# The carry of the causal convolution between two halves: made from PSUM in the first half and entered as the bias of ACT's first tap

## The chip, the cores and the metric

The kernel runs on one core of one Trainium2 chip. The metric is the device time of one execution in microseconds (us); lower is better. The engines are TensorE (PE; its weight loads are PEld), VectorE (DVE), ScalarE (ACT), GpSimd (POOL) and SyncE (SP), which issues most of the DMAs.

## The reference

One layer on 1024 tokens of 512 features, in float32: adaptive layer norm, a Mamba-2 block with 128 heads of 64 and 8 groups, its gated and normed output projection, and then a layer norm with a feed-forward product by the signs of the weights. What matters here is the causal convolution of four taps over tokens, one filter per channel, on x (8192 channels) and on B and C (1024 channels each):

```python
proj = jnp.einsum('bsd,ed->bse', x, in_proj_w)
gate = proj[..., :INTER]
hBC = proj[..., INTER:INTER + CONV_DIM]
xc = jnp.transpose(hBC, (0, 2, 1))
xc = jax.lax.conv_general_dilated(xc, conv_w, (1,), [(K - 1, 0)], ..., feature_group_count=CONV_DIM)
xc = xc + conv_b[None, :, None]
hBC = jax.nn.silu(jnp.transpose(xc, (0, 2, 1)))
hs, Bm, Cm = ...
...
Y = (Y_diag + Y_off).reshape(b, s, H, P) + hs * D[None, None, :, None]
g = y * jax.nn.silu(gate)
```

Token t of a channel becomes w3 x[t] + w2 x[t-1] + w1 x[t-2] + w0 x[t-3] + bias.

## The kernel before, in words

Channels lie on the 128 partitions, tokens along the free dimension. The 1024 tokens are two halves of 512 (HALF), and the 8192 channels of x are 16 blocks of 512 (four tiles of 128 channels, j = 0 to 3). A **unit** is one block and one half. A group holds two blocks, so four units: c = 0 (first block, first half), c = 1 (first block, second half), c = 2 and c = 3 (the second block). The 8 groups run as a loop on each engine, with the first and last written apart. All engines run programs of their own, ordered by semaphores; the order on each engine is written out by hand.

A product of float32 values is made from high and low parts, as three matmuls for each of 4 slices: one projection of a tile is 12 matmuls of 128x512 (`split_product`, lines 449 to 451) into one bank of PSUM.

The work is pipelined by a unit. While unit u computes decays, states and outputs in four steps j, TensorE also projects the four tiles of x for unit u + 1 (`project_step`), and ACT and DVE convolve them. So a unit on a first half (c = 0, 2) convolves the second half of its block, and a unit on a second half (c = 1, 3) the first half of the next block. With c = 3 also four items of the next group's B and C go with them (bc0 and bc1: B, first and second half; bc2 and bc3: C). For an item:

- ACT's `tap` (lines 828 and 838) reads the bank and writes the first tap, w3 x + bias, over all 512 columns into xc (or bt, craw). For a first half it also copies the last three columns of the bank into `tail` or `bctail` (lines 827, 837). It waits for the projection and for line 1329, which reads the old xc (`v_t2`).
- DVE's `conv` (line 1118) adds three wide taps out of the bank, of 511, 510 and 509 columns. In a second half it adds three short taps of 1, 2 and 3 columns from `tail`: what the last three tokens of the first half contribute. Each operation waits for the one before (`v_taps`), as they write the same tensor.
- ACT applies SiLU to xc (line 926), and TensorE transposes it for the next unit (line 648).

In each step j DVE does: two multiplications of lm by the mask (line 1304, after ACT's decays of lines 980 and 983), yt (1329, after TensorE's product of line 734), ea (1334), the low part of g of the step before (1311), and the convolution of item j. POOL follows with yt (1487, after ea), the gate (1490), the sum of squares (1482) and the low part of one weight tile (1418). ACT splits weights (810), copies ea (988), makes g's high part (1000) and the squares (1007), and evicts the gates with SiLU (939).

Of the gate projections (`gate_proj`), that of tile 0 for the next unit stands in step j = 2, after the last tile of x. Tiles 1 and 2 open the next unit: tile 1 waits for the third convolution (`v_conv`, as its bank is the one of that item), tile 2 for the SiLU of tile 0, and the transposes for the SiLU of all four tiles of xc. The output projection of the unit before follows the first transposes.

## Time and profile before

| what | value |
| --- | --- |
| median of 3 runs | 1948.02 us (1947.24 to 1951.38) |
| span of the profiled execution | 1944.2 us |
| time of the profiled execution with what lies around the span | not given apart; the median is 3.8 us above the span |
| TensorE busy | 1828.1 us, 94% |
| DVE busy | 1392.7 us, 72% |
| ACT busy | 1011.6 us, 52% |
| POOL busy | 925.6 us, 48% |
| mean granted clock of TensorE | 0.981 |
| DMA | 114.18 MB, mean 59 GB/s |

The span runs from the first to the last instruction. The busy time of TensorE is modelled at its ends, so 94% does not mean that it works at its peak. In the rows below an instruction is given as line, engine, operation, output<-inputs by the program's names, and shape. "[1.78 <-DVE xc L1118]" is idle time of the engine before it and what ended that. Times in a timeline are us from the start of the span, and neighbours of one kind are merged (x3), so their length is that of the row from first start to last end.

### The profile page before, as it was taken

How to read it: one execution, taken by the hardware profiler on the slowest of the kernel's cores; microseconds unless marked ns; L12 is line 12 of the kernel's file. 1: busy time of each engine (PE TensorE's matmuls, PEld its weight loads, DVE VectorE, ACT ScalarE, POOL GpSimd, SP SyncE). 2: the span in 40 equal slices, each digit the busy share in tenths (PEclk: the TensorE clock that was granted, in tenths of full speed). 3: DMA queues.
4: the chain of work that ended last, by engine and by line, in shares of the span. 5: the costliest groups of instructions: out<-in, count | busy, mean ns of one | idle time of the engine just before them, and what ended most of it. 6: DMA issues, size and time to landing. Idle time of an engine off the chain costs nothing.

```text
span 1944.2 us, 31172 instructions
## 1 busy us (share of the span) xinstructions
PE 1828.1 (94%) x9752; PEld 1410.3 (73%) x9752; DVE 1392.7 (72%) x2094; ACT 1011.6 (52%) x1775; POOL 925.6 (48%) x717
## 2 busy tenths in 40 slices
PE   7899999999999989999999999999999999999966
PEld 6767777777777768677777777777677777777745
DVE  5876677767766677866677677666777667776788
ACT  5455544555645555555445555455555555455532
POOL 1245454545534464454545545354554545454564
PEclk9799999999999999999999999999999999999988
DMA  5412121111202121021211212111211212111121
GB/s 180 154 32 69 53 63 42 46 60 50 66 30 69 44 65 50 28 69 53 63 43 45 61 44 69 32 64 47 67 50 29 64 59 63 42 46 60 33 88 58
DMA packets 76397, 114.18 MB, mean 59 GB/s; under 512 B 21696, under 2 KB 27328, under 8 KB 75328
## 3 DMA queue, kind: packets, MB, share of 16 engines
q1 hardware_dynamic: 58656, 80.07, 13.7%
q10 hardware_dynamic: 17568, 31.99, 4.9%
q8 instruction: 86, 1.41, 0.3%
q14 instruction: 87, 0.71, 0.1%
HBM read 88.94 MB, written 23.07 MB: 58 GB/s over the span
## 4 chain that ended last, share of the span: by engine, by line
PE 40%; DVE 21%; issue 19%; POOL 11%; ACT 6%; DMA 1%; SPq 0%; POOLq 0%; DVEq 0%; ACTq 0%
DVE xc L1118 11%; PE bank L449 9%; PE bank L451 9%; PE bank L450 9%; PE bank L586 3%; POOL yt L1487 3%; POOL wg_lo L1418 3%; PE bank L734 2%; POOL wx_lo L1418 2%; PE bank L648 2%; PE bank L601 1%; PE bank L721 1%; ACT lm L980 1%; PE bank L612 1%; DVE ea L1334 1%
## 5 line engine op out<-in xcount | busy, mean ns | idle before, releaser
L1487 POOL TENSOR_TENSOR yt<-yt,ea 128x384 f32<-128x384 f32 (+1 forms) x128 | 189.6, 1481 | 464.8 <-DVE ea L1334 464.8
L1118 DVE SCALAR_TENSOR_TENSOR xc<-bank,bpar,xc 128x511 f32<-128x511 f32 (+2 forms) x384 | 286.1, 747 | 43.4 <-ACT xc L838 34.2
L449 PE MATMUL bank<-h_hi,wg_hi 128*128 128x512 f32 x640 | 265.5, 415 | 39.3 <-DVE xc L1118 36.1
L1304 DVE TENSOR_TENSOR lm<-lm,cbm 128x512 f32<-128x512 f32 x256 | 173.3, 718 | 164.9 <-ACT lm L983 164.9
L451 PE MATMUL bank<-h_hi,wg_lo 128*128 128x512 f32 x640 | 255.3, 399 | 0.0
L450 PE MATMUL bank<-h_lo,wg_hi 128*128 128x512 f32 x640 | 255.0, 398 | 0.0
L449 PE MATMUL bank<-h_hi,wx_hi 128*128 128x512 f32 x512 | 211.1, 412 | 2.5 <-DVE bt L1118 1.3
L449 PE MATMUL bank<-wo_hi,g_hi 128*128 128x512 f32 x496 | 206.4, 416 | 0.0
L1468 POOL TENSOR_TENSOR prev<-prev,dec 128x512 f32<-128x512 f32 x96 | 101.9, 1061 | 215.0 <-DVE prev L1253 131.8
L450 PE MATMUL bank<-h_lo,wx_hi 128*128 128x512 f32 x512 | 201.4, 393 | 0.0
L451 PE MATMUL bank<-h_hi,wx_lo 128*128 128x512 f32 x512 | 200.9, 392 | 0.0
L451 PE MATMUL bank<-wo_hi,g_lo 128*128 128x512 f32 x496 | 194.9, 393 | 0.0
L450 PE MATMUL bank<-wo_lo,g_hi 128*128 128x512 f32 x496 | 193.6, 390 | 0.0
L939 ACT ACTIVATE gate<-bank 128x512 f32<-128x512 f32 x128 | 75.2, 588 | 210.7 <-PE bank L451 97.8
L988 ACT ACTIVATE ea<-bank 128x512 f32<-128x512 f32 x128 | 76.3, 596 | 202.4 <-PE bank L612 163.5
L449 PEld LDWEIGHTS bank<-h_hi,wg_hi 128*128 128x128 f32 x640 | 123.7, 193 | 75.4 <-DVE xc L1118 43.3
L1490 POOL TENSOR_TENSOR yt<-yt,gate 128x512 f32<-128x512 f32 x128 | 166.1, 1298 | 10.0
L1482 POOL TENSOR_TENSOR ssq<-ssq,sq 128x512 f32<-128x512 f32 x112 | 145.1, 1295 | 26.3 <-ACT sq L1007 26.3
L838 ACT ACTIVATE xc<-bank,bpar 128x512 f32<-128x512 f32 x128 | 99.4, 776 | 102.8 <-DVE yt L1329 59.3
L983 ACT ACTIVATE lm<-lm 128x512 f32<-128x512 f32 x256 | 148.9, 644 | 0.0
L734 PE MATMUL bank<-lm,xdt 128*64 128x128 f32 x2048 | 140.9, 280 | 6.8 <-DVE acc L1223 6.3
L451 PEld LDWEIGHTS bank<-h_hi,wg_lo 128*128 128x128 f32 x640 | 123.5, 193 | 28.1
(180 smaller groups left out, 3858.0 us busy)
## 6 DMA issues: line engine op xcount, KB each, us to landing
raw_w<-w_in_dram SPq DMA_DIRECT2D x145, 256.0 KB, 2.6
raw_w<-w_out_dram SPq DMA_DIRECT2D x64, 256.0 KB, 2.6
part_d<-part ACTq DMA_DIRECT2D x64, 256.0 KB, 2.4
part<-part_d ACTq DMA_DIRECT2D x58, 256.0 KB, 2.7
rt<-rows_d SPq DMA_DIRECT2D x256, 8.0 KB
acc<-x_dram SPq DMA_DIRECT2D x8, 256.0 KB, 6.8
acc<-w_mod_dram SPq DMA_DIRECT2D x2, 1024.0 KB, 6.5
lh<-neg_d SPq DMA_DIRECT2D x128, 8.0 KB
```

Of the source, the lines that this page charges most:

```text
L449: nc.tensor.matmul(out_ap, whi(k), hhi(k), start=(k == 0), stop=False)
L450: nc.tensor.matmul(out_ap, whi(k), hlo(k), start=False, stop=False)
L451: last = nc.tensor.matmul(out_ap, wlo(k), hhi(k), start=False, stop=(k == n - 1))
L734: lst = nc.tensor.matmul(bank[5][64 * i:64 * i + 64, chunk(z)], xdt[:, z, h * HDIM:(h + 1) * HDIM], lm[:, h % 4, chunk(z)], start=True, st ...
L838: act(xc[:, j, :], bank[b][:, :], ACT.Identity, bias=par(parity, j, CONV_B), scale=par(parity, j, TAPS - 1)).then_inc(a_tap, 1)
L983: act(lm[:, h % 4, :], lm[:, h % 4, :], ACT.Exp, scale=-1.0).then_inc(a_l, 1)
L1118: stt(dst[:, at], src, w(k), dst[:, at], ALU.mult, ALU.add)\
L1304: tt(lm[:, h % 4, :], lm[:, h % 4, :], cbm[:, toks(hf)], ALU.mult).then_inc(v_m, 1)
L1468: tt(prev[:, slot(hf, z + 1), :].rearrange("p (h c) -> p h c", h=BH), prev[:, slot(hf, z), :].rearrange("p (h c) -> p h c", h=BH), d.unsqu ...
L1482: tt(ssq[:, hf, :], ssq[:, hf, :], sq[:, :], ALU.add).then_inc(p_ss, 1)
L1487: tt(yt[:, j % 2, cols], yt[:, j % 2, cols], ea[:, j % 2, cols], ALU.add).then_inc(p_t3, 1)
L1490: tt(yt[:, j % 2, :], yt[:, j % 2, :], gate[:, j, :], ALU.mult).then_inc(p_g, 1)
```

## The change

In the first half DVE itself now makes from the bank what the last three tokens add to the first three of the second half, with the bias: w0 x on three columns (a tensor_scalar with the bias), then w1 x on two and w2 x on one, each interleaved with a wide tap. In the second half ACT makes the first tap of columns 0, 1 and 2 one at a time, with that column of `tail` as per-partition bias, and then the other 509 columns with the plain bias. ACT's copy of three columns is gone, and so are DVE's three short taps of the second half. ACT's tap of a second half gets a wait for the convolution of the same tile in the first half. The counters of links between DVE's operations change with the order (`taps_before`, `BC_TAPS`).

```diff
--- before.py
+++ after.py
@@ -186,10 +186,10 @@
             return 7 * nb + 4 * hf
 
         def taps_before(nb, hf, j):
-            return 28 * nb + (8 + 5 * j if hf else 2 * j)
+            return 28 * nb + (20 + 2 * j if hf else 5 * j)
         def squares_before(g, c):
             return 14 * g + (0, 3, 6, 10)[c]
-        BC_TAPS = (0, 2, 7, 9)
+        BC_TAPS = (0, 5, 7, 12)
 
 
         W_SLOTS = {"x": (wx_hi, wx_lo), "g": (wg_hi, wg_lo), "o": (wo_hi, wo_lo)}
@@ -823,9 +823,14 @@
                     if j == 0:
                         se.wait_ge(d_bcpar, 16 * (gg + 1))
                         ge(se, t_st, 14 * gg)
-                    if h2 == 0:
-                        act(bctail[:, m, :], bank[b][:, HALF - 3:HALF], ACT.Copy)
-                    act((bt, craw)[m][:, toks(h2)], bank[b][:, :], ACT.Identity, bias=bcp(m, CONV_B),
+                    o, first = (bt, craw)[m][:, toks(h2)], 0
+                    if h2 == 1:
+                        se.wait_ge(v_bcconv, 4 * gg + j)
+                        first = TAPS - 1
+                        for t in range(first):
+                            act(o[:, t:t + 1], bank[b][:, t:t + 1], ACT.Identity, bias=bctail[:, m, t:t + 1],
+                                scale=bcp(m, TAPS - 1))
+                    act(o[:, first:HALF], bank[b][:, first:HALF], ACT.Identity, bias=bcp(m, CONV_B),
                         scale=bcp(m, TAPS - 1)).then_inc(a_bctap, 1)
                     return
                 v = 2 * nb + hf
@@ -833,9 +838,14 @@
                 if j == 0 and hf == 0:
                     se.wait_ge(d_bpar, 16 * (nb + 1))
                 ge(se, v_t2, 4 * (v - 1) + j + 1)
-                if hf == 0:
-                    act(tail[:, j, :], bank[b][:, HALF - 3:HALF], ACT.Copy)
-                act(xc[:, j, :], bank[b][:, :], ACT.Identity, bias=par(parity, j, CONV_B),
+                first = 0
+                if hf == 1:
+                    se.wait_ge(v_conv, 4 * (v - 1) + j + 1)
+                    first = TAPS - 1
+                    for t in range(first):
+                        act(xc[:, j, t:t + 1], bank[b][:, t:t + 1], ACT.Identity, bias=tail[:, j, t:t + 1],
+                            scale=par(parity, j, TAPS - 1))
+                act(xc[:, j, first:HALF], bank[b][:, first:HALF], ACT.Identity, bias=par(parity, j, CONV_B),
                     scale=par(parity, j, TAPS - 1)).then_inc(a_tap, 1)
 
             def scale_h(s, scale, shift, halves=(0, 1)):
@@ -1109,14 +1119,22 @@
                     ve.wait_ge(a_tap, 4 * v + j + 1)
                     done, link, n0 = v_conv, v_tap, taps_before(nb, hf, j)
                 ps = bank[b]
-                steps = [(slice(3 - k, HALF), ps[:, 0:HALF - 3 + k], k) for k in (2, 1, 0)]
-                if h2:
-                    steps += [(slice(0, 3 - k), tl[:, k:3], k) for k in (2, 1, 0)]
-                for r, (at, src, k) in enumerate(steps):
-                    if r:
-                        ve.wait_ge(link, n0 + r)
-                    stt(dst[:, at], src, w(k), dst[:, at], ALU.mult, ALU.add)\
-                        .then_inc(done if r == len(steps) - 1 else link, 1)
+                for r, k in enumerate((2, 1, 0)):
+                    if h2:
+                        if r:
+                            ve.wait_ge(link, n0 + r)
+                    else:
+
+                        n = 3 - r
+                        if r:
+                            ve.wait_ge(link, n0 + 2 * r - 1)
+                            stt(tl[:, 0:n], ps[:, HALF - n:HALF], w(r), tl[:, 0:n], ALU.mult, ALU.add).then_inc(link, 1)
+                            ve.wait_ge(link, n0 + 2 * r)
+                        else:
+                            ts(tl[:, 0:n], ps[:, HALF - n:HALF], w(r), w(CONV_B), ALU.mult, ALU.add).then_inc(link, 1)
+                    at = slice(3 - k, HALF)
+                    stt(dst[:, at], ps[:, 0:HALF - 3 + k], w(k), dst[:, at], ALU.mult, ALU.add)\
+                        .then_inc(done if r == 2 else link, 1)
 
 
             acc_tile = lambda t: acc[:, t, :]
```

### How instructions move

DVE, second half, in the first unit of the program (c = 0), step j = 1, before. The rows are instructions in program order; `t_yd`, `a_tap` and so on are the semaphores waited for; `tail` holds the last three tokens of the first half, `bpar` the weights of the convolution. Line 1329 makes yt, line 1334 ea, line 1311 the low part of g, line 1118 is the convolution:

```order
L1329 SCALAR_TENSOR_TENSOR yt<-xc,bpar,bank 128x512 [waits t_yd]
L1334 TENSOR_TENSOR ea<-bank,ea 128x384 [waits a_ea,t_yo]
L1311 SCALAR_TENSOR_TENSOR g_lo<-yt,bpar,g_hi 128x512 [waits a_hi]
L1118 SCALAR_TENSOR_TENSOR xc<-bank,bpar,xc 128x511 [waits a_tap]
L1118 SCALAR_TENSOR_TENSOR xc<-bank,bpar,xc 128x510 [waits v_taps]
L1118 SCALAR_TENSOR_TENSOR xc<-bank,bpar,xc 128x509 [waits v_taps]
L1118 SCALAR_TENSOR_TENSOR xc<-tail,bpar,xc 128x1 [waits v_taps]
L1118 SCALAR_TENSOR_TENSOR xc<-tail,bpar,xc 128x2 [waits v_taps]
L1118 SCALAR_TENSOR_TENSOR xc<-tail,bpar,xc 128x3 [waits v_taps]
L1304 TENSOR_TENSOR lm<-lm,cbm 128x512 [waits a_l] x2
```

The same place now (the lines are 1347, 1352, 1329, 1136 and 1322 in the changed file):

```order
L1347 SCALAR_TENSOR_TENSOR yt<-xc,bpar,bank 128x512 [waits t_yd]
L1352 TENSOR_TENSOR ea<-bank,ea 128x384 [waits a_ea,t_yo]
L1329 SCALAR_TENSOR_TENSOR g_lo<-yt,bpar,g_hi 128x512 [waits a_hi]
L1136 SCALAR_TENSOR_TENSOR xc<-bank,bpar,xc 128x511 [waits a_tap]
L1136 SCALAR_TENSOR_TENSOR xc<-bank,bpar,xc 128x510 [waits v_taps]
L1136 SCALAR_TENSOR_TENSOR xc<-bank,bpar,xc 128x509 [waits v_taps]
L1322 TENSOR_TENSOR lm<-lm,cbm 128x512 [waits a_l] x2
```

The three short taps on `tail` behind the wide ones are gone, and the next multiplication of lm follows the last wide tap.

DVE, first half, in the second unit (c = 1), step j = 0, before:

```order
L1329 SCALAR_TENSOR_TENSOR yt<-xc,bpar,bank 128x512 [waits v_lo,a_sq,t_yd]
L1334 TENSOR_TENSOR ea<-bank,ea 128x512 [waits a_ea,t_yo]
L1118 SCALAR_TENSOR_TENSOR xc<-bank,bpar,xc 128x511 [waits a_tap]
L1118 SCALAR_TENSOR_TENSOR xc<-bank,bpar,xc 128x510 [waits v_taps]
L1118 SCALAR_TENSOR_TENSOR xc<-bank,bpar,xc 128x509 [waits v_taps]
L1304 TENSOR_TENSOR lm<-lm,cbm 128x512 [waits a_l] x2
```

and now:

```order
L1347 SCALAR_TENSOR_TENSOR yt<-xc,bpar,bank 128x512 [waits v_lo,a_sq,t_yd]
L1352 TENSOR_TENSOR ea<-bank,ea 128x512 [waits a_ea,t_yo]
L1134 TENSOR_SCALAR tail<-bank,bpar 128x3 [waits a_tap]
L1136 SCALAR_TENSOR_TENSOR xc<-bank,bpar,xc 128x511
L1131 SCALAR_TENSOR_TENSOR tail<-bank,bpar,tail 128x2 [waits v_taps]
L1136 SCALAR_TENSOR_TENSOR xc<-bank,bpar,xc 128x510 [waits v_taps]
L1131 SCALAR_TENSOR_TENSOR tail<-bank,bpar,tail 128x1 [waits v_taps]
L1136 SCALAR_TENSOR_TENSOR xc<-bank,bpar,xc 128x509 [waits v_taps]
L1322 TENSOR_TENSOR lm<-lm,cbm 128x512 [waits a_l] x2
```

A short operation that makes or adds to `tail` stands ahead of each wide tap, and the first of them takes the wait for ACT's tap.

ACT, second half, in the first unit, steps j = 0 and 1, before. Line 838 is the wide first tap, line 810 a weight split, line 988 the copy of ea, lines 980 and 983 the decays, line 1000 the high part of g:

```order
L838 ACTIVATE xc<-bank,bpar 128x512 [waits v_t2,t_x]
L810 ACTIVATE wo_hi<-raw_w 128x512 [waits d_w1,d_scr]
L988 ACTIVATE ea<-bank 128x512 [waits p_t3,t_ea]
L980 ACTIVATE lm<-bank 128x512 [waits t_yd,t_diff] x2
L983 ACTIVATE lm<-lm 128x512 [waits a_fall] x2
L1000 ACTIVATE g_hi<-yt,bpar 128x512 [waits d_scr,p_g]
```

and now (lines 846 and 848 the taps, 998 ea, 990 and 993 the decays, 1010 g):

```order
L846 ACTIVATE xc<-bank,tail,bpar 128x1 [waits v_conv,v_t2,t_x]
L846 ACTIVATE xc<-bank,tail,bpar 128x1 x2
L848 ACTIVATE xc<-bank,bpar 128x509
L810 ACTIVATE wo_hi<-raw_w 128x512 [waits d_w1,d_scr]
L998 ACTIVATE ea<-bank 128x512 [waits p_t3,t_ea]
L990 ACTIVATE lm<-bank 128x512 [waits t_yd,t_diff] x2
L993 ACTIVATE lm<-lm 128x512 [waits a_fall] x2
L1010 ACTIVATE g_hi<-yt,bpar 128x512 [waits d_scr,p_g]
```

Three one-column taps with `tail` as bias stand ahead of the wide one, which has three columns fewer, and the first of them also waits for the convolution of the first half.

## Rows read from the trace of the kernel before

**Rows 1.** The waits: engine, line, waited for, us, times, longest.

```profile
PE bank L449 <- DVE xc L1118: 36.1, 16, 2.8
PE bank L648 <- ACT xc L926: 18.4, 20, 1.8
```

**Rows 2.** Timeline of TensorE: start, length (us), line, operation, [idle before]; c = 2, c = 0.

```profile
917.52 0.39 PE L449 MATMUL bank<-h_hi,wg_hi 128*128 128x512 f32 x1
920.24 0.83 PE L721 MATMUL bank<-ct,prev 128*128 128x128 f32 x6
921.00 1.09 PE L734 MATMUL bank<-lm,xdt 128*64 128x128 f32 x16
...
924.83 0.57 PE L449 MATMUL bank<-h_hi,wg_hi 128*128 128x512 f32 x1 [2.73 <-DVE xc L1118]
932.37 0.65 PE L648 MATMUL bank<-ident,xc 128*128 128x128 f32 x4 [0.19 <-ACT xc L926]
...
1048.23 0.50 PE L449 MATMUL bank<-h_hi,wg_hi 128*128 128x512 f32 x1 [1.78 <-DVE xc L1118]
1055.76 0.65 PE L648 MATMUL bank<-ident,xc 128*128 128x128 f32 x4 [1.78 <-ACT xc L926]
```

**Rows 3.** Timeline of DVE, unit with c = 2.

```profile
914.11 2.73 DVE L1118 SCALAR_TENSOR_TENSOR xc<-tail,bpar,xc 128x1 f32<-128x1 f32 x3
...
924.69 0.74 DVE L1329 SCALAR_TENSOR_TENSOR yt<-xc,bpar,bank 128x512 f32<-128x512 f32 x1
```

**Rows 4.** Groups of DVE: form, count, busy us, mean ns, idle before.

```profile
L1118 DVE SCALAR_TENSOR_TENSOR xc<-tail,bpar,xc 128x1 f32<-128x1 f32 x64 | 62.5, 976 | 2.3
...
L1118 DVE SCALAR_TENSOR_TENSOR craw<-bctail,bcpar,craw 128x1 f32<-128x1 f32 x8 | 10.1, 1264 | 0.3
...
L1118 DVE SCALAR_TENSOR_TENSOR bt<-bctail,bcpar,bt 128x1 f32<-128x1 f32 x8 | 1.8, 219 | 0.3
```

**Rows 5.** Timeline of POOL, unit with c = 2.

```profile
914.03 1.28 POOL L1482 TENSOR_TENSOR ssq<-ssq,sq 128x512 f32<-128x512 f32 x1
...
925.98 1.45 POOL L1487 TENSOR_TENSOR yt<-yt,ea 128x384 f32<-128x384 f32 x1 [1.48 <-DVE ea L1334]
...
930.00 1.30 POOL L1418 TENSOR_TENSOR wo_lo<-raw_w,wo_hi 128x512 fp32r<-128x512 f32 x1
```

**Rows 6.** Line 1118, wide taps: min/median/max ns.

```profile
L1118 DVE SCALAR_TENSOR_TENSOR xc<-bank,bpar,xc x384: 736/748/752, 79.5 to 1836.5; 128x511 f32<-128x511 f32 x64, 128x509 f32<-128x509 f32 x64, 128x510 f32<-128x510 f32 x64
```

**Rows 7.** Timeline of DVE, a small operation out of PSUM.

```profile
936.60 0.16 DVE L1229 TENSOR_SCALAR rstd<-bank 128x4 f32<-128x4 f32 x1 [2.25 <-PE bank L557]
```

**Rows 8.** Groups of ACT: form, count, busy us, mean ns.

```profile
L838 ACT ACTIVATE xc<-bank,bpar 128x512 f32<-128x512 f32 x128 | 99.4, 776 | 102.8 <-DVE yt L1329 59.3 <-PE bank L451 43.5
...
L988 ACT ACTIVATE ea<-bank 128x512 f32<-128x512 f32 x128 | 76.3, 596 | 202.4 <-PE bank L612 163.5 <-POOL yt L1487 27.9 <-DVE part L1214 11.0
...
L837 ACT ACTIVATE tail<-bank 128x3 f32<-128x3 f32 x64 | 10.9, 170 | 69.2 <-PE bank L451 58.2 <-DVE yt L1329 11.0
```

**Rows 9.** Timeline of ACT, last step of the unit with c = 2.

```profile
925.52 0.78 ACT L838 ACTIVATE xc<-bank,bpar 128x512 f32<-128x512 f32 x1 [1.59 <-DVE yt L1329]
926.20 0.62 ACT L810 ACTIVATE wo_hi<-raw_w 128x512 fp32r<-128x512 f32 x1
926.72 0.58 ACT L939 ACTIVATE gate<-bank 128x512 f32<-128x512 f32 x1
```

**Rows 10.** Timeline of DVE, unit with c = 3.

```profile
972.61 4.53 DVE L1118 SCALAR_TENSOR_TENSOR craw<-bank,bcpar,craw 128x511 f32<-128x511 f32 x6
977.18 1.78 DVE L1118 SCALAR_TENSOR_TENSOR craw<-bctail,bcpar,craw 128x1 f32<-128x1 f32 x3
...
982.97 0.68 DVE L1334 TENSOR_TENSOR ea<-bank,ea 128x512 f32<-128x512 f32 x1
```

**Rows 11.** Timeline of TensorE, unit with c = 3.

```profile
984.10 1.05 PE L721 MATMUL bank<-ct,prev 128*128 128x128 f32 x8
```

**Rows 12.** Window behind the pause: length, TensorE busy (x), granted clock, DMA.

```profile
924.80:928.30 3.50, 3.48 (x9) 0.55 0.24 75
```


## The prediction

> **What bounds the kernel now.** First the waits of TensorE. Its matmuls stand idle 36.1 us in 16 places for DVE's convolution and 18.4 us for ACT's SiLU of xc [rows 1]. Sixteen is the number of units that work on a first half (c = 0 and c = 2 in each of 8 groups); in these units the second half of the block is projected and convolved. So I went to one of them, c = 2 of a middle group. The last product of the unit (line 734) starts at 921.00 and ends at 922.09. Call that end T. The next gate projection waits until 924.83 for the third convolution, and the transposes of xc start at 932.37, T + 10.28 [rows 2]. Between them lie only two gate projections. One takes 920.24 - 917.52 = 2.72 us at full clock [rows 2], so 5.4 us of the 10.3 are work. In a unit with c = 0 the first pause is 1.78 us: T = 1046.45, and the transposes start at T + 9.31 [rows 2].
>
> What DVE does there is the second reading. It has no idle time in the steps j = 1 to 3. The three short taps behind three wide ones, of 1, 2 and 3 columns, take 2.73 us together [rows 3]. Over the run the one-column tap on xc has a mean of 976 ns, on bt 219, on craw 1264 [rows 4]. The same instruction is up to six times as long in some places, with nothing before it to wait for, so it waits inside itself. POOL's timeline says for what: one of its operations runs from 914.03 to 915.31 [rows 5] and the first short tap is issued at 914.11. The wide taps meet the same POOL traffic and never differ: 736 to 752 ns in 384 [rows 6]. They read one input from PSUM and one from SBUF; the short ones read both from SBUF. So a DVE operation with two SBUF inputs waits for the POOL operation in progress, and one with a PSUM input does not. The Trainium skill, "SBUF — State Buffer", section "SBUF: two separate sides", calls the pair of ports that DVE and GpSimd share an exclusive lock, held for a whole instruction and asked for by a DVE operation with two SBUF inputs; by that rule, the trace agrees, at 219 against 1264 ns.
>
> **The change, DVE in the second half.** Three short taps go per item, 240 in all. Three cost 0.66 us where POOL is idle (3 x 219 ns [rows 4]) and up to 2.73 where it is busy [rows 3]. Of these items 64 lie in units with c = 0 or 2, and two per group in c = 3.
>
> **DVE in the first half.** As many short operations come in, 240. Each has a PSUM input, so by [rows 6] none should wait for POOL. The nearest row is a 4-column operation out of PSUM, 0.16 us [rows 7]. They stand between wide taps that wait for one another anyway, so part of them fits into those gaps; I take 0.3 us per item. The ends are 0.1 (almost all of it fits) and 0.67 (three times the 0.22 of a short tap). They lie in units with c = 1 (4 items) and c = 3 (6 items).
>
> **ACT.** The 3-column copy of the first half (0.17 us [rows 8], 80 of them) goes, off the path. In the second half three one-column taps come ahead of the wide one, 240 in all. Their price is not in the trace. A wide tap with two per-partition operands takes 776 ns, a plain read of PSUM of the same width 596 [rows 8]: 0.18 us for the operands, which I take to be the same at any width. So a short tap takes 0.17 + 0.18 = 0.35. Consecutive ACT instructions overlap by 0.10 (0.78 + 0.62 us of work between 925.52 and 926.72 [rows 9]), so 0.25 each, and d = 0.75 us for three. Ends: 3 x 0.07 = 0.21 (operands free) and 3 x 0.35 = 1.05 (no overlap). The Trainium skill, "ScalarE: Activation LUTs", section "What ACT_TABLE_LOAD costs", gives 186 ns, 93 per pointer operand, 0.83 per column and an overlap of 93. By that, an estimate, d would be 0.84 and the gain 16 x 0.09 = 1.4 us less; its 93 per operand agrees with the 0.18 of the rows, the short taps no run here shows.
>
> **The path after.** DVE saves about 2 us in each of the steps j = 1 and j = 2, although ACT's tap, which must wait for yt (line 1329) and is now d longer, becomes what DVE waits for (about 0.6 us a step). The third convolution, over at 924.8 now, ends at about 921, before T, and the first pause is gone. Late next is the second gate projection. Its bank needs the SiLU of the first gate, and that stands on ACT behind the tap of item 3. From T: yt takes 0.74 (924.69 to 925.43) and ACT's tap starts 0.09 later [rows 3, 9]; tap, weight split and SiLU of the gate take 926.72 + 0.58 - 925.52 = 1.78 [rows 9], and d comes on top. That makes T + 2.7 + d with the hops, while the first gate projection ends at T + 2.72. TensorE therefore idles about d, restarts (0.2, the first matmul 0.57 us for 0.39 [rows 2]) and projects 2.72: transposes at T + 5.6 + d = T + 6.35. The convolution of item 3 and its SiLU are ready by about T + 5.5, so they are not last. POOL's lower part of the last weight, 5.32 us after the step's first POOL work (925.98 to 930.00 + 1.30 [rows 5]), which starts some 1.3 us after T, comes at T + 6.7, just when the out projection behind the transposes wants it. So a smaller d gains little.
>
> Gain per unit: 10.28 - 6.35 = 3.9 with c = 2, 9.31 - 6.35 = 3.0 with c = 0. Times 8 each: 55 us.
>
> **What it costs elsewhere.** In c = 3, the tap of bc3 now waits for the convolution of bc2, with x0's tap and the next decays queued behind it on ACT. Six wide taps and three short ones take DVE from 972.61 to 977.18 + 1.78 = 978.96 [rows 10]. After: bc2 to 975.2, then ACT 0.75 + 0.78, bc3 from 976.8 to 979.1. The short taps saved pay for the wait, and DVE comes 0.2 to 1.2 us later to x0 and to what follows. TensorE takes the product with prev at 984.10 [rows 11] and needs DVE's ea for it, ready at 982.97 + 0.68 = 983.65 [rows 10]. So 0 to 0.8 us per group; I take 0.3, 2 us in all. The prologue has the same waits once: its taps come about 4 us later on ACT while DVE and TensorE there wait for other things, so 0, within 2. Nothing moves on SP, and on POOL only the times do.
>
> Sum: 55 - 2 = 53. Against the profiled span of 1944.2 us: 1891. The median of the runs, 1948.0, holds 3.8 us more than that span; 1948.0 - 53 = 1895.
>
> **Rivals.** *Half-speed clock.* Behind the pause at 924.83 the granted clock was 0.55 for 3.5 us, with 9 matmuls where 15 fit [rows 12]: TensorE's lower level of 1.2 GHz. Today this is hidden in the wait for DVE. If the shorter pauses still bring it on in all 16 units, 1.7 us each, the gain is 53 - 27 = 26, 1922; in half of them, 1908. Against it: behind the pause of 1.78 us at 1048.23 TensorE was early enough to stand idle 1.78 us once more before the transposes [rows 2], so it ran at full clock. *Other chains.* The weight split on POOL and its loads, or c = 3, hold the later units, and half of the gain arrives: 1921. For it: POOL works for 5.3 us in one go in the last step of c = 2 [rows 5]. Against: its work starts from events of DVE that come earlier as well. *All of it absorbed:* within 0.2%. *Slower.* The short operations of the first half wait for POOL in spite of their PSUM input, because their other input and their output are in SBUF. Then c = 1 gets the stall that c = 2 loses, about 4 us, and c = 3, already the fullest and with six such items for four, 12: 16 per group, 128 in all, less 53: 75 us slower would be 2023 if nothing hid any of it. DVE waits for others in both, which I put at half: 64 - 53 = 11, 1959. It decides from 6.6 us per group on. Against it stand 384 wide taps of 736 to 752 ns with the same kinds of operands [rows 6].
>
> **How the numbers follow.** Forecast (both pauses shrink as worked out) 0.70, clock 0.11, half absorbed 0.10, all absorbed 0.03, slower 0.03, and 0.03 for a larger gain, if c = 3 becomes faster too. The forecast's own range: d from 1.05 to 0.21 moves the gain by -5 and +2 (POOL); c = 3 and the prologue by -6 to +4; a few places of slow clock by -5. That is 1889 to 1911. The excess over 5.4 us of work is 4.8 and 3.9 us per unit, 70 us in all; losing all of it would give 1878, and no more is to be had in these places. I reach down to 1881 and, for the milder forms of the clock and of absorption, up to 1914. A measurement of this kernel tells about 0.2%, 4 us. Faster 0.94, within 0.2% 0.03, slower 0.03.
>
> **What would show it.** No DVE tap of 1 to 3 columns near 1.2 us, all near 0.2; ACT's one-column taps at 0.35; the wait of line 449 for the convolution near zero, and a new one of about 0.7 us for ACT's gate; DVE waiting for ACT's tap. It is wrong if short taps take over 0.4 us in c = 1 or 3, if pauses of TensorE turn up there, or if slow matmuls follow every short pause.

## The result and the profile after

| | before | after |
| --- | --- | --- |
| median of 4 runs, us | 1948.64 (1947.24 to 1951.38) | 1912.92 (1912.19 to 1919.00) |
| ratio to before, 95% interval | | 0.9824 (0.9807 to 0.984) |
| span of the profiled execution, us | 1944.2 | 1917.2 |
| busy, us: TensorE, DVE | 1828.1, 1392.7 | 1828.7, 1294.0 |
| busy, us: ACT, POOL | 1011.6, 925.6 | 1061.2, 938.7 |

Faster by 35.7 us where 53 were forecast; 1912.9 lies in the range, near its upper end. The profiled execution of after is the one of 1919.0 us: beside 1.8 us around its span it holds some 6 us more than the median, and so its unit times below make the change look a little worse than the medians do.

The waits of TensorE in the changed kernel (engine, line, waited for: us, times, longest). The first row of before [rows 1], 36.1 us, is gone, and so is most of its second. Two waits stand in their place: the one for ACT's gate, which was 2.0 us before, and the one for POOL's lower part of the output weight, which is new. The wait for DVE's xw comes once, at the start (0.9 us before); the one for the accumulation was there already (6.3).

```profile
PE bank L449 <- ACT gate L949: 13.9, 21, 1.2
...
PE bank L734 <- DVE acc L1241: 7.8, 7, 1.3
PE bank L449 <- POOL wo_lo L1436: 6.1, 16, 0.5
PE bank L586 <- DVE xw L1294: 5.1, 1, 5.1
```

The groups of DVE that answer to [rows 4] (form, count, busy us, mean ns, idle before): the one-column tap of 976 ns and the one of 1264 are now 208 and 209. The first short operation, a tensor_scalar, is dearer than the others.

```profile
L1134 DVE TENSOR_SCALAR tail<-bank,bpar 128x3 f32<-128x3 f32 x64 | 17.6, 274 | 11.1 <-ACT xc L848 11.1
L1131 DVE SCALAR_TENSOR_TENSOR tail<-bank,bpar,tail 128x2 f32<-128x2 f32 x64 | 13.4, 210 | 0.0
L1131 DVE SCALAR_TENSOR_TENSOR tail<-bank,bpar,tail 128x1 f32<-128x1 f32 x64 | 13.3, 208 | 0.0
...
L1131 DVE SCALAR_TENSOR_TENSOR bctail<-bank,bcpar,bctail 128x1 f32<-128x1 f32 x16 | 3.3, 209 | 0.0
```

The short operations also never differ much, which a mean can't tell: line 1131 over the whole run, min/median/max ns, first and last start. Of all 240 short operations of the changed kernel 200 overlap an operation of POOL, and the longest takes 283 ns.

```profile
L1131 DVE SCALAR_TENSOR_TENSOR tail<-bank,bpar,tail x128: 199/209/218, 81.9 to 1759.1; 128x2 f32<-128x2 f32 x64, 128x1 f32<-128x1 f32 x64
```

The same groups of ACT, the row that the prediction had no price for, and the wide tap beside it:

```profile
L846 ACT ACTIVATE xc<-bank,tail,bpar 128x1 f32<-128x1 f32 x192 | 53.5, 347 | 73.7 <-PE bank L451 58.0 <-DVE yt L1347 10.1 <-issue 5.5
L848 ACT ACTIVATE xc<-bank,bpar 128x509 f32<-128x509 f32 x64 | 50.0, 781 | 0.0
```

TensorE in the same unit with c = 2 as in [rows 2] (start, length, line, operation, idle before). Line 734 ends at 914.01; the first gate projection follows at once, the second after a pause of 0.66, the transposes 6.72 us after T, and then there is a pause that was not there before.

```profile
912.92 1.09 PE L734 MATMUL bank<-lm,xdt 128*64 128x128 f32 x16
914.16 0.51 PE L449 MATMUL bank<-h_hi,wg_hi 128*128 128x512 f32 x1
...
917.88 0.50 PE L449 MATMUL bank<-h_hi,wg_hi 128*128 128x512 f32 x1 [0.66 <-ACT gate L949]
...
920.73 0.60 PE L648 MATMUL bank<-ident,xc 128*128 128x128 f32 x4
921.80 0.50 PE L449 MATMUL bank<-wo_hi,g_hi 128*128 128x512 f32 x1 [0.47 <-POOL wo_lo L1436]
```

ACT in the last step of that unit, which answers to [rows 9]: three one-column taps take 0.82 us and the wide one starts 0.71 after the first of them.

```profile
915.33 0.82 ACT L846 ACTIVATE xc<-bank,tail,bpar 128x1 f32<-128x1 f32 x3
916.04 0.78 ACT L848 ACTIVATE xc<-bank,bpar 128x509 f32<-128x509 f32 x1
916.70 0.64 ACT L810 ACTIVATE wo_hi<-raw_w 128x512 fp32r<-128x512 f32 x1
917.22 0.60 ACT L949 ACTIVATE gate<-bank 128x512 f32<-128x512 f32 x1
```

### Where the time went, unit by unit

The repeating measure of this kernel is the time from a unit's first transposes (line 648) to the next unit's. Read off TensorE's timeline, as the mean of the six units of groups 2 to 7, in us (1 to 9 are the experiments below; the last column is when the second unit's transposes start, which measures the prologue):

| kernel | c = 0 | c = 1 | c = 2 | c = 3 | second transposes |
| --- | --- | --- | --- | --- | --- |
| before | 54.73 | 50.64 | 55.00 | 66.90 | 146.24 |
| after | 51.68 | 51.15 | 51.44 | 68.87 | 151.38 |
| 1 short taps from PSUM | 51.14 | 51.71 | 51.06 | 67.26 | 143.06 |
| 2 B and C as before | 51.69 | 51.16 | 51.48 | 68.10 | 143.18 |
| 3 POOL's order, all steps | 52.35 | 50.65 | 53.38 | 67.40 | 152.38 |
| 4 prologue | 51.69 | 51.16 | 51.47 | 67.93 | 145.39 |
| 5 ACT's taps twice | 52.71 | 50.61 | 52.98 | 68.51 | 152.17 |
| 6 carry by DVE | 51.02 | 51.83 | 50.95 | 67.68 | 143.18 |
| 7 carry by DVE, POOL's last step | 51.02 | 50.72 | 50.95 | 67.62 | 143.07 |
| 8 POOL's last step | 51.68 | 50.60 | 51.46 | 67.60 | 151.30 |
| 9 prologue, POOL's last step | 51.70 | 50.60 | 51.44 | 67.49 | 143.53 |

The units with c = 0, 1 and 2 repeat within 0.1 us from group to group, except those with c = 2 in experiment 3 (52.7 to 54.3); c = 3 doesn't. Its seven units took 65.1, 67.4, 67.0, 68.7, 66.2, 67.0 and 65.2 before and 65.8, 68.2, 69.9, 68.6, 70.0, 68.4 and 68.1 after.

From before to after the last first-transposes of a unit come 27.7 us earlier (1840.74 to 1813.01). The single units sum to it: c = 0 (7) -21.2, c = 2 (8) -28.2, c = 1 (8) +4.0, c = 3 (7) +12.6, and the way to the second transposes +5.1, though it holds a unit with c = 0 that should have given 3.05 as well, so the start costs 8.2. The span's difference is 27.0, less than the 35.7 of the medians: the profiled execution of before lies 2.6 us under its median, that of after 6.1 above.

Part of what c = 3 adds is TensorE's clock. In after, three of its seven units (69.9, 70.0 and 68.1) hold a stretch of 3.4 us at a granted clock of 0.5, the lower of its two levels (1.2 GHz), which costs 1.7 us each; in before one has it (68.7). Without these stretches the mean of groups 2 to 7 is 66.6 before and 68.0 after.

### The profile page after: what moved, and what is told of

Same layout as the page of the kernel before. It is cut to its first block, busy times and chain, and to the rows that moved or that the text cites. A ratio compares the mean times of both kernels' runs of the same rounds, so it can differ in the third digit from the quotient of the medians.

```text
span 1917.2 us, 31312 instructions
## 1 busy us (share of the span) xinstructions
PE 1828.7 (95%) x9752; PEld 1408.7 (73%) x9752; DVE 1294.0 (67%) x2094; ACT 1061.2 (55%) x1935; POOL 938.7 (49%) x717
## 4 chain that ended last, share of the span: by engine, by line
issue 45%; POOL 33%; PE 12%; DVE 4%; ACT 2%; DMA 1%; SPq 1%; POOLq 1%; ACTq 0%; DVEq 0%
POOL yt L1505 9%; POOL ssq L1500 6%; POOL wg_lo L1436 4%; POOL wo_lo L1436 4%; POOL prev L1486 3%; POOL yt L1508 3%; POOL wx_lo L1436 3%; PE bank L449 3%; PE bank L451 2%; PE bank L450 2%; PE bank L586 1%; PE bank L479 1%; PE bank L734 1%; PE bank L648 1%; PE bank L782 0%
## 5 line engine op out<-in xcount | busy, mean ns | idle before, releaser
L1322 DVE TENSOR_TENSOR lm<-lm,cbm 128x512 f32<-128x512 f32 x256 | 186.1, 768 | 164.5 <-ACT lm L993 164.5
L1486 POOL TENSOR_TENSOR prev<-prev,dec 128x512 f32<-128x512 f32 x96 | 101.8, 1061 | 220.7 <-DVE prev L1271 132.3
L1436 POOL TENSOR_TENSOR wx_lo<-raw_w,wx_hi 128x512 fp32r<-128x512 f32 x64 | 89.6, 1406 | 126.7 <-ACT wx_hi L810 126.7
L1436 POOL TENSOR_TENSOR wg_lo<-raw_w,wg_hi 128x512 fp32r<-128x512 f32 x80 | 112.6, 1408 | 78.4 <-ACT wg_hi L810 78.4
```

Of the source, the lines that this page charges most:

```text
L1322: tt(lm[:, h % 4, :], lm[:, h % 4, :], cbm[:, toks(hf)], ALU.mult).then_inc(v_m, 1)
L1436: tt(lo[:, j, :], raw_w[:, s, :], hi[:, j, :].bitcast(F), ALU.subtract).then_inc(p_w, 1)
L1486: tt(prev[:, slot(hf, z + 1), :].rearrange("p (h c) -> p h c", h=BH), prev[:, slot(hf, z), :].rearrange("p (h c) -> p h c", h=BH), d.unsqu ...
```

## The experiments

Before each comes the text on record; times are medians of 4 runs, with the ratio to the kernel before and its 95% interval. The kernel before was timed again beside each set: 1947.51 (1943.95 to 1955.35) with experiments 1 to 4, 1949.51 with 5 to 8, 1949.31 with 9. The changed kernel was not, so a difference between kernels of different sets is uncertain by the 2 us between these medians, beside the spread of the runs.

### 1. The kernel before, with the short taps of the second half reading PSUM

```diff
-                    steps += [(slice(0, 3 - k), tl[:, k:3], k) for k in (2, 1, 0)]
+                    steps += [(slice(0, 3 - k), ps[:, 0:3 - k], k) for k in (2, 1, 0)]
```

> The kernel before, with one edit: the three short taps of a second half read their first input from the first columns of the bank (PSUM) in place of tail (SBUF). Their number, place, order and output stay. It leaves out what the first half's last tokens contribute (wrong columns are added), so only its time is of use. Theory (a DVE operation with two SBUF inputs waits for the POOL operation in progress): all short taps take about 0.22 us, none 1.2; a unit from transposes to transposes takes 51.2 to 51.8 us with c = 0 and 51.2 to 51.8 with c = 2 (54.7 and 55.0 before), c = 1 stays at 50.6 to 51.2, and the total comes to 1890 to 1900 us. Rival (short operations behind wide ones that they depend on are slow by themselves, or their number counts): one-column taps keep a mean near 1 us and the total stays at 1944 to 1950.

Measured: 1901.43 us (1899.25 to 1905.77), ratio 0.9765 (0.9732 to 0.9798). This kernel is only good for timing, since it adds wrong columns. No instruction is added or moved; only where one operand lies has changed. The one-column tap on xc went from 976 [rows 4] to 219 ns:

```profile
L1118 DVE SCALAR_TENSOR_TENSOR xc<-bank,bpar,xc 128x1 f32<-128x1 f32 x64 | 14.0, 219 | 2.3
```

So the stall needs the second SBUF operand, and its removal alone is worth 46 us. The trace of before shows, over all 240 short taps, that what they waited for was POOL. 96 of them are long, and each ends 12 to 20 ns after the POOL operation that it overlaps; 143 overlap none and take 219 to 224 ns, and one meets the last 36 ns of one and takes 219. Here 167 of the 240 lie wholly inside a POOL operation, and none takes more than 224 ns. TensorE's largest wait is now for POOL's lower part of the output weight:

```profile
PE bank L449 <- POOL wo_lo L1418: 13.1, 16, 0.9
```

With nothing added on ACT and a yet earlier DVE, this wait is longer than in the changed kernel (6.1): what POOL does in the last step is the next thing late.

### 2. The changed kernel, with the items of B and C convolved as before

The counters `BC_TAPS`, ACT's copy and DVE's six taps are those of before for B and C; x stays as changed. The cut core, in DVE's `conv`:

```diff
+                if kind == "bc":
+                    steps = [(slice(3 - k, HALF), ps[:, 0:HALF - 3 + k], k) for k in (2, 1, 0)]
+                    if h2:
+                        steps += [(slice(0, 3 - k), tl[:, k:3], k) for k in (2, 1, 0)]
...
```

> The changed kernel, with the items of B and C (bt, craw) handled as before the change: ACT copies the last three columns, taps all 512, DVE makes the short taps from SBUF; x stays as changed. Theory (the new wait of ACT's tap of bc1 and bc3 for DVE's convolution costs in two places: in the prologue it holds up the weight splits and with them SP's stores, about 7 us once; in c = 3 it makes DVE and ACT late, about 0.7 us per group, felt by TensorE at the gate of the next group): the second transposes start near 144 instead of 151, the wait of TensorE for ACT's gate at a group's start falls from about 1 us to 0.5, total 1899 to 1902 against 1912.5. Rival (c = 3 is longer because of POOL and the clock alone, and the prologue differs by chance): total 1910 to 1914.

Measured: 1907.61 (1904.92 to 1909.62), 0.9791 (0.9759 to 0.9823). The start is as it should be (second transposes 143.18, 8.2 earlier than in the changed kernel), so the cost at the start comes with the items of B and C. c = 3 came to 68.10 with the wait for POOL still in it. The time fell by 5.3 us, less than the 8.2 at the start and less than was expected; 2.5 of the 8.2 lie ahead of the first transposes, where single executions differ (see experiments 4 and 9).

### 3. POOL's lower part of the weight ahead of its sum of squares, in every step of c = 0 and c = 2

```diff
+                    for f in (todo[j:j + 1] if hf == 0 else []):
+                        unit_fill(f, g)
...
-                    for f in todo[j:j + 1]:
+                    for f in (todo[j:j + 1] if hf == 1 else []):
```

> The changed kernel, with POOL's low part of the weight put ahead of the sum of squares in units on a first half (c = 0, 2). Theory (the 0.5 us more in c = 1 and 0.67 in c = 3 are the out projection waiting for that low part): c = 1 goes from 51.15 to 50.65 us, c = 3 falls by about 0.67, no wait of line 449 for wo_lo is left, total 8 x 1.17 = 9 us less, 1903. Rival (the late squares then hold up ACT's next square or the sum of squares, or the wait only moves to the transposes or the gate): 1910 to 1915.

Measured: 1929.21 (1927.91 to 1930.68), 0.99 (0.9869 to 0.993): 16.3 us slower than the change, where the theory had 9 us faster and the rival at most 1915. The wait for the weight is gone (c = 1 at 50.65), but the one for the gate has doubled, since ACT now stands still in front of its squares, which need POOL's sum, and the one-column taps and the gate's SiLU are queued behind them. TensorE's wait, and ACT's timeline in the last step of c = 2:

```profile
PE bank L449 <- ACT gate L949: 28.1, 21, 2.0
```

```profile
923.54 0.63 ACT L1017 ACTIVATE sq<-yt 128x512 f32<-128x512 f32 x1 [1.23 <-POOL ssq L1500]
924.08 0.82 ACT L846 ACTIVATE xc<-bank,tail,bpar 128x1 f32<-128x1 f32 x3
```

The pause for the gate in c = 2 is now 1.95 us, and behind it the slow clock of the prediction's rival comes back: in five of the eight units with c = 2 a stretch at half speed follows, and these take 53.9 to 54.4 us; the other three stay at full clock and take 52.7. Two of these stretches, with and without (length, busy of PE, PEld, DVE, ACT and POOL, clock, DMA):

```profile
1374.40:1377.90 3.50, 3.47 (x17) 2.92 (x18) 2.36 (x3) 3.27 (x6) 2.67 (x3) 1.00 0.29 75
1820.10:1823.60 3.50, 3.50 (x9) 2.76 (x10) 2.26 (x3) 3.19 (x6) 2.76 (x3) 0.51 0.00 0
```

### 4. The prologue: two weight splits of ACT ahead of the tap of bc3

```diff
+            se.wait_ge(t_bc, 4)
+            pro_split(7, 9)
...
-
-                    se.wait_ge(t_bc, 4)
-                    pro_split(7, FILLS0)
+                    pro_split(9, FILLS0)
```

> The changed kernel, where ACT's splits of the first two gate weights in the prologue stand ahead of the tap of bc3, which waits for DVE, and no longer behind it. Theory (that wait delayed the splits from about 71 to 79 us, with them SP's next weight loads and the stores of the rows queued behind these, and so the first loads of the unit's parameters): SP's stores start 3 to 8 us earlier, the idle time of TensorE before the states of the first unit (5.07 us) goes, total 1905 to 1909. Rival (the first unit waits for DVE's own convolutions, which are later): the stores start earlier but the total stays within 2 us of 1912.5.

Measured: 1908.25 (1906.72 to 1909.87), 0.9793 (0.9762 to 0.9824). Here is the cost that the prediction put at nothing. In the changed kernel ACT waits 3.77 us for DVE's convolution of bc2, with the splits behind it (an earlier tap, that of bc1, waits 7.93 us for bc0's convolution in the same way):

```profile
76.63 0.83 ACT L831 ACTIVATE craw<-bank,bctail,bcpar 128x1 f32<-128x1 f32 x3 [3.77 <-DVE craw L1136]
...
78.67 1.16 ACT L810 ACTIVATE wg_hi<-raw_w 128x512 fp32r<-128x512 f32 x2
```

The splits, and POOL's lower parts that follow them, free the buffers into which SP loads the next weights, and on SP's queue the stores of the decays come behind these loads, one after another in order. SP before, and after:

```profile
72.84 1.56 SPq L286 DMA_DIRECT2D raw_w<-w_in_dram  x2
74.52 2.49 SPq L352 DMA_DIRECT2D rows_d<-g_hi  x4
```

```profile
80.70 1.56 SPq L286 DMA_DIRECT2D raw_w<-w_in_dram  x2
82.38 2.48 SPq L352 DMA_DIRECT2D rows_d<-g_hi  x4
```

These loads and stores of SP are 7.86 us later, and the last stores 8.6. DVE then waits for the decays, and TensorE for DVE: 5.07 us in the changed kernel, 0.94 with the splits moved. Behind the longer pause the granted clock of TensorE is 0.53 for 3.5 us, so that the first two matmuls take 2.08 us for 1.12; behind the shorter one it is 1.00.

```profile
109.73 2.08 PE L586 MATMUL bank<-xw,bt 128*128 128x512 f32 x2 [5.07 <-DVE xw L1294]
```

```profile
105.32 1.12 PE L586 MATMUL bank<-xw,bt 128*128 128x512 f32 x2 [0.94 <-DVE xw L1294]
```

The second transposes moved from 151.38 to 145.39. Of the 8.2 us this mends 6.0, although the wait before the tap of bc3 itself is not touched (2.73 us there). From the first to the second transposes the changed kernel takes 47.75 us, this one 42.05 and experiment 2 42.09: here the cost is mended whole. The rest of the 8.2 lies ahead of the first transposes, which start at 103.62 in the changed kernel, 103.34 here and 101.09 in experiment 2.

### 5. ACT's one-column taps made twice

Each one-column tap is followed by a second one into a scratch column, with the same operands.

```diff
+                        act(small[:, 57 + t:58 + t], bank[b][:, t:t + 1], ACT.Identity, bias=tail[:, j, t:t + 1],
+                            scale=par(parity, j, TAPS - 1))
```

> The changed kernel with ACT's three one-column taps each made twice, the second time into a scratch column: 480 in place of 240, 0.73 us more per second-half item. Theory (TensorE's wait for the SiLU of the gate in c = 0 and c = 2 is the length of these taps): that wait grows from 0.43 and 0.70 to about 1.2 and 1.4 us; POOL's weight part, which TensorE waited for behind it (0.31 and 0.46), is then in time, so c = 0 and c = 2 grow by 0.7 each and c = 1 and c = 3 shrink by about 0.5; net 16 x 0.2 to 16 x 0.4 = 3 to 6 us: 1915 to 1919. Rival (ACT has slack here, the wait belongs to something else): waits and time unchanged, 1911 to 1914. Rival (each us of ACT costs a us of the end): 16 x 0.73 = 12 us and more, 1924 or above.

Measured: 1933.75 (1928.89 to 1935.06), 0.9913 (0.9884 to 0.9942). 20.8 us for 240 more instructions of 0.25 us each (start to start; 60 us of ACT's time), where the theory had 3 to 6; its second rival, 12 us and more, comes nearer. A unit with c = 0 grew by 1.03 us and one with c = 2 by 1.54, where ACT's taps of one step grew by about 0.75: in c = 2 the delays of earlier steps reach TensorE as well, by a second wait that the changed kernel does not have there, that for DVE's xc (1.02 us a unit). The wait for ea belongs to c = 3.

```profile
PE bank L449 <- ACT gate L953: 26.4, 21, 1.4
...
PE bank L721 <- DVE ea L1356: 9.9, 9, 3.1
PE bank L449 <- DVE xc L1140: 8.8, 11, 1.0
```

So 0.75 us more on ACT in each of the four steps costs TensorE 1.0 to 1.5 us a unit, 1.4 to 2 times what one step adds and not four times. In the other direction this holds down to the point where another wait ends last; the next kernel asks where that is.

### 6. The carry entered by DVE

ACT's one-column taps and its wait for the convolution are taken out: its tap of a second half has 509 columns. DVE, whose three wide taps there had no short ones left, makes the first three columns in one operation, w3 x (from PSUM) + tail.

```diff
-                    se.wait_ge(v_conv, 4 * (v - 1) + j + 1)
...
-                    for t in range(first):
-                        act(xc[:, j, t:t + 1], bank[b][:, t:t + 1], ACT.Identity, bias=tail[:, j, t:t + 1],
-                            scale=par(parity, j, TAPS - 1))
...
+                if h2:
+                    ve.wait_ge(link, n0)
+                    stt(dst[:, 0:3], ps[:, 0:3], w(TAPS - 1), tl[:, 0:3], ALU.mult, ALU.add).then_inc(link, 1)
```

> The changed kernel with the carry entered by DVE in place of ACT: ACT's tap of a second half makes 509 columns, without its one-column taps and without its wait for the first half, and DVE makes the first three columns in one short operation, w3 times the bank (PSUM) plus tail (SBUF), ahead of the wide taps. Theory: TensorE's wait for the gate (0.43 and 0.70 us) goes, c = 0 and c = 2 take about 51.1, and the time comes back in c = 1 and c = 3 as a longer wait for POOL's wo_lo (0.8 in place of 0.31 and 0.46), as in the run with PSUM inputs; what is left is the prologue, where ACT no longer waits: about 6 us less than the changed kernel, 1905 to 1909. Rival (ACT's taps cost more than the gate's wait shows): below 1900.

Measured: 1902.95 (1902.32 to 1903.89), 0.976 (0.9736 to 0.9785), 10.0 us below the change and some 2 below what was expected. As ACT waits for no convolution here, the prologue is mended too, and the fairer comparison is with experiment 2, from which it differs by 4.7 us. The pause for the gate is all but gone (0.2 at most) and c = 0 and c = 2 are at 51.02 and 50.95, but the wait for POOL took most of it back (c = 1 at 51.83):

```profile
PE bank L449 <- POOL wo_lo L1430: 15.0, 16, 1.0
```

### 7. The same, and POOL's weight ahead of its sum in the last step alone

```diff
+                    ahead = hf == 0 and j == 3
+                    for f in (todo[j:j + 1] if ahead else []):
+                        unit_fill(f, g)
...
-                    for f in todo[j:j + 1]:
+                    for f in ([] if ahead else todo[j:j + 1]):
```

> The run with the carry entered by DVE, and POOL's low part of the weight put ahead of the sum of squares in the last step (j = 3) of units on a first half alone. Theory: POOL's last piece was the floor; now the wait of line 449 for wo_lo goes in c = 1 and c = 3, c = 1 takes 50.65, c = 3 about 0.8 less, and c = 0 and c = 2 stay at 51.1: about 8 x (1.06 + 0.8) = 15 us less than with the carry alone, 1888 to 1894. Rival (as with the reorder in all steps, ACT's square waits for POOL's sum and holds the gate's SiLU): the wait for ACT's gate is above 1 us and the total over 1905.

Measured: **1887.69** (1886.58 to 1891.99), 0.9679 (0.9655 to 0.9703). It beats both kernels: 62 us below before, 25 below the change. In the last step no tap is queued behind ACT's squares, so what undid experiment 3 doesn't happen. POOL's weight ends at 904.69, before the transposes at 904.85, where in the changed kernel it ended 1.01 after their start (920.02 + 1.72 against 920.73):

```profile
903.39 1.30 POOL L1430 TENSOR_TENSOR wo_lo<-raw_w,wo_hi 128x512 fp32r<-128x512 f32 x1
904.64 1.74 POOL L1494 TENSOR_TENSOR ssq<-ssq,sq 128x512 f32<-128x512 f32 x1
```

Neither the gate nor the weight is left among TensorE's larger waits; first in the loop stands the accumulation in c = 3:

```profile
PE bank L734 <- DVE acc L1235: 8.8, 7, 1.5
```

### 8. The changed kernel with POOL's last step reordered

The diff of experiment 7 for POOL, on the changed kernel, ACT's taps as they are.

> The changed kernel with the reorder of POOL in the last step (j = 3) of units on a first half alone. In the run with the reorder in all steps the wait for wo_lo went and that for ACT's gate grew from 0.43 and 0.70 to 1.07 and 1.95 us. Theory (that growth came from the steps before the last, where ACT's square of the step waits for POOL's sum and stands ahead of the tap): here the gate's wait stays at 0.43 and 0.70, c = 1 takes 50.65 and c = 3 is 0.67 shorter: 9 us less than the changed kernel, 1902 to 1905. Rival (the last step alone holds up ACT too): 1912 or above.

Measured: 1906.26 (1905.56 to 1909.85), 0.9782 (0.9757 to 0.9808). c = 0 and c = 2 are as in the changed kernel, c = 1 fell from 51.15 to 50.60. The wait for POOL cost 0.55 us a unit in c = 1, with a record of 0.31. The record is too small because matmuls overlap: here the first one of the output projection starts 0.35 us after the first transpose, while the last transpose is still on record until 0.60; in the changed kernel it starts at 0.91.

### 9. Both repairs

The changed kernel with the edits of experiments 4 and 8.

> The changed kernel with both repairs: the weight splits of the prologue ahead of bc3's tap, and POOL's lower part of the last weight ahead of its sum of squares in step j = 3 of c = 0 and c = 2. Theory: the two costs lie in different places (once in the prologue, 8 times in each of c = 1 and c = 3), so they add: 4.7 us and 6.7 us off 1912.9, 1901 to 1903, with the second transposes near 145.4, c = 1 near 50.6 and c = 3 near 67.6. Rival: the repairs share slack, or c = 3 is longer for a reason of its own that grows again: 1905 to 1908, and c = 3 at 68 or above without a wait for the output weight.

Measured: 1898.64 (1897.08 to 1899.74), 0.9739 (0.9717 to 0.9761), 14.3 us below the change and lower than expected. The second transposes came at 143.53, not 145.4: the first ones were at 101.49 instead of 103.34, a shift that the two edits don't explain. Single executions do differ by this much at the start: with the changed kernel's prologue the first transposes are at 103.62, 103.79 (experiment 8), 104.08 (3) and 101.65 (5), and with the repaired one at 103.34 (4) and 101.49. All five kernels whose ACT does not wait for B and C have them at 101.1 to 101.8. What decides it stays open, and with it whether these 2 us belong to the change.

## Why the prediction was right, and where it was wrong

The steps of the prediction that failed are three terms beside the main one: the prologue at 0 (it cost 8.2 us), POOL's weight just in time, so at 0 as well (6.7), and c = 3 at 2 us (7.5 to 12.6, in part the same wait for POOL). The mechanism and the main term, 55 us, held.

**Right: what stalled, and why.** Experiment 1 shows it without the rest of the change: with one operand of the short taps in PSUM instead of SBUF the stalls are gone, and in before every stalled tap ends with POOL's operation. The Trainium skill, "SBUF — State Buffer", section "SBUF: two separate sides", has DVE operations with two SBUF inputs ask for the lock; by that rule, experiment 1 agrees, at 219 to 221 ns for every form against 976 [rows 4]. The rival "slower", short operations that wait for POOL in spite of their PSUM input, fell with a longest time of 218 ns among 128. One reading was off without a consequence: in the step j = 1 of c = 2 DVE does have a pause, of 1.36 us, ahead of the multiplications of lm at 908.77.

**Right: the two gains.** Transposes came at T + 6.72 in c = 2, for T + 6.35 forecast; per unit 3.56 us for 3.9. In c = 0 the gain was 3.05 for 3.0. Over 16 units these make 52.9 us of the 55. ACT's price held: 347 ns for 350 and d = 0.71 for 0.75; the idle behind the first gate projection was 0.66 and 0.43. The short operations of DVE's first half cost 0.2 us an item where 0.3 were taken. The Trainium skill, "ScalarE: Activation LUTs", section "What ACT_TABLE_LOAD costs", would have 186 + 93 + 93 + 1 = 373 ns and 0.84 for three, an estimate from its figures; the trace has 347 and 0.71. The rival of the half-speed clock fell too: in no unit with c = 0 or c = 2 after the first did the granted clock fall below 1.00. It was near, as experiment 3 shows with its pauses of 1.95 us. In the unit above, the two stretches behind the pauses read (window: length, busy of PE, PEld, DVE, ACT and POOL, clock, DMA):

```profile
914.00:917.70 3.70, 3.07 (x14) 2.18 (x12) 3.38 (x6) 3.70 (x10) 3.62 (x4) 1.00 0.05 13
917.90:920.70 2.80, 2.80 (x12) 2.29 (x13) 2.24 (x3) 2.80 (x6) 2.80 (x3) 1.00 0.14 55
```

**Wrong: POOL "just when the out projection behind the transposes wants it".** The working took POOL's 5.32 us from a start of 1.3 us after T. But POOL had no gap left to start from: its first work of the step follows the last of the one before without a pause (idle 1.48 us before it in [rows 5], none now), at T + 1.96, and takes 5.77.

```profile
914.71 1.31 POOL L1436 TENSOR_TENSOR wo_lo<-raw_w,wo_hi 128x512 fp32r<-128x512 f32 x1
915.97 1.47 POOL L1505 TENSOR_TENSOR yt<-yt,ea 128x384 f32<-128x384 f32 x1
...
920.02 1.72 POOL L1436 TENSOR_TENSOR wo_lo<-raw_w,wo_hi 128x512 fp32r<-128x512 f32 x1
```

It ends at T + 7.73, 1.0 us later than worked out. Of that, 0.4 is the stall of the prediction from the other side. POOL's last operation takes 1.72 us for the usual 1.30, because it meets DVE's g_lo, an operation with two SBUF inputs, in progress, and ends 1.13 us after it; that one in turn had started during POOL's sum of squares and takes 1.00 us (0.74 at 910.56, with no POOL operation in progress):

```profile
918.77 1.29 POOL L1500 TENSOR_TENSOR ssq<-ssq,sq 128x512 f32<-128x512 f32 x1
919.61 1.00 DVE L1329 SCALAR_TENSOR_TENSOR g_lo<-yt,bpar,g_hi 128x512 fp32r<-128x512 f32 x1 [0.44 <-ACT g_hi L1010]
```

All 16 of these places have it (1.72 to 1.74 us, the end 1.13 to 1.14 after that of g_lo), and eight more with a multiplication of lm in progress; in before none of the 65 operations on wo_lo took more than 1.31. The wait of TensorE falls behind the transposes, so into the next unit's time, 0.5 us in c = 1 and, by the longer record, some 0.6 in c = 3. Its 16 places make about 9 us, and taking it away gave 6.7 (experiment 8). That "a smaller d gains little" held only as long as POOL's order did: with the prologue mended, taking the taps off ACT gained 4.7 us (experiment 6 against 2), and 11.0 where POOL's last step was reordered as well (7 against 9; the last transposes in their profiled executions differ by 7.0).

**Wrong: the prologue "0, within 2".** It cost 8.2 us in the profiled execution, of which the 5.7 from the first to the second transposes belong to the change for certain. The working said that the taps come later while DVE and TensorE wait for other things. It followed ACT's taps to their own readers and left out what else is queued on ACT behind the waiting tap: weight splits, whose buffers SP's loads wait for, with the stores of the decays behind them. Where I wrote "Nothing moves on SP", no instruction did, but its loads and stores there came 7.9 us later. Two moved splits mended 6.0 of it, and 4.7 us of the median.

**Too small: c = 3, "0.3 per group".** In the profiled execution of after it is 1.97 a unit, of which the weight's wait is some 0.6 and the slow clock (three such stretches in six units, one before) another 0.6. The pause for the gate at the end of the unit grew, which the items of bc2 and bc3 on ACT bring with them (0.61 in experiment 2). In the middle of the run, before and after:

```profile
998.17 0.47 PE L449 MATMUL bank<-h_hi,wg_hi 128*128 128x512 f32 x1 [0.54 <-ACT gate L939]
```

```profile
1210.69 0.47 PE L449 MATMUL bank<-h_hi,wg_hi 128*128 128x512 f32 x1 [1.01 <-ACT gate L949]
```

That is 0.47 more, where the working looked at DVE's ea and the product of line 721 alone. With the weight's wait away (experiments 8 and 9) c = 3 is 0.6 to 0.7 above before. Experiment 4, which has the same loop as after and no slow stretch in it, gave 67.93. Line 734 waits for DVE's accumulation in all seven of these units of both kernels (0.4 to 1.4 us before, 0.5 to 1.3 after); a stretch at half clock follows it in some (at 955.86 before, granted clock 0.52; at 1167.76 after, 0.52) and not in others (at 944.9 after, 1.00). What decides it stays open; even the kernels of experiments 1, 6 and 7 are 0.4 to 0.8 above before in c = 3.

**The sum again.** 52.9 from c = 0 and c = 2, less 4 in c = 1, less 8.2 at the start, less 7.5 in c = 3 (experiment 4's seven units against before's) makes 33; measured 35.7. With the two terms that I had put at nothing repaired, the kernel takes 1898.6, where the forecast was 1895.0: what was wrong were these side terms, not the mechanism. That 33 comes so near to 35.7 is partly luck: the first three terms use the profiled execution of after, which is 6 us above its median.

## What to carry to other kernels

Where a small DVE operation takes several times its price with nothing to wait for, see whether it ends each time with an operation of another engine, and move one of its inputs to PSUM; here this alone, with no instruction moved, gave 46 us of 1948 (in a kernel with wrong columns, good for timing only). When an instruction gets a new wait, write down everything that stands behind it on its engine and what each of these frees, as far as the DMA queue that reuses the buffer. And when a stall goes, don't time the next engine from its old start: look whether it still has a pause there, and try the smallest reordering of it, in the one step where its result is late, since the same reordering in all steps cost 16 us here. Put two operations of these two engines that both take their inputs from SBUF apart in time where one of them is late.

## What was unexpected of the hardware

- An operation of one column, a few bytes per partition, stood for more than 1 us inside itself. How long it stood went by POOL's operation, with which it ended within 20 ns, and not by its own size. The same happened to POOL, whose wo_lo took 1.72 us for 1.30 behind an operation of DVE with two SBUF inputs.
- A tensor_scalar with two per-partition operands on three columns out of PSUM took 274 ns, a scalar_tensor_tensor on three columns 221 (experiment 1) and on two 210: the form counted more than the columns.
- Three short operations of 0.70 us together cost DVE 0.19 us between wide taps that wait for one another: a convolution with them takes 2.50 us (513.30 to 515.80), one without them 2.31. The gaps of a chain of dependent operations had room for them. DVE's timeline in c = 3 of the changed kernel:

```profile
513.30 0.28 DVE L1134 TENSOR_SCALAR bctail<-bank,bcpar 128x3 f32<-128x3 f32 x1
...
514.28 0.74 DVE L1136 SCALAR_TENSOR_TENSOR craw<-bank,bcpar,craw 128x510 f32<-128x510 f32 x1
514.94 0.21 DVE L1131 SCALAR_TENSOR_TENSOR bctail<-bank,bcpar,bctail 128x1 f32<-128x1 f32 x1
515.06 0.74 DVE L1136 SCALAR_TENSOR_TENSOR craw<-bank,bcpar,craw 128x509 f32<-128x509 f32 x1
517.43 2.31 DVE L1136 SCALAR_TENSOR_TENSOR craw<-bank,bcpar,craw 128x511 f32<-128x511 f32 x3 [1.63 <-ACT craw L833]
```
